# The last two attention iterations and the routing of batches 0 and 1 in another order, and GpSimd leaving its branch one step earlier

## The chip, the cores and the metric

The kernel runs on one core of a Trainium2 chip. The metric is the device time of one execution in microseconds (us). The time quoted for a kernel is the median of several executions, and one further execution is recorded by the hardware profiler; its span is the time from the first to the last instruction.

## The reference

One transformer layer over 16 batches of 256 tokens and 128 features, in float32. An attention block with a small MLP is followed by a mixture of 32 experts of which each token takes 4:

```python
h = layernorm(x) * (1 + ca) + sa
xn = rms_norm(h, ln1_w); q, k, v = xn @ Wq, xn @ Wk, xn @ Wv       # q, k normalised per head, 16 heads of 8
attn = softmax((einsum('bqhd,bkhd->bhqk', q, k) + rel_bias) * scale, causal)
y = einsum('bhqk,bkhd->bqhd', attn, v) @ Wo + h
z = relu(rms_norm(y, ln2_w) @ W1) @ W2                              # 128 -> 512 -> 128
x = x + ga * (z + y)
h = layernorm(x) * (1 + cb) + sb
scores = sigmoid(h @ gate_w.T)                                      # 32 experts
ids = top_k(scores + e_bias, 4); w = scores[ids] / sum(scores[ids])
x = x + gb * sum_k w_k * ((silu(h @ w1[e]) * (h @ w3[e])) @ w2[e])
```

## The kernel before

The program gives each of the five engines one instruction list, written by hand in program order, and the lists meet only at semaphores. An engine that waits holds up everything behind it in its own list. The order of calls in the source is the order of execution.

The work has four stages.

**Attention.** One call of `sequence(b, ...)` on each engine handles one batch of 16. The scores of a batch come as eight units (two heads each), issued by TensorE in four `pair` calls; VectorE adds the bias (`add_pair`, line 1528), ScalarE exponentiates (`exp`, line 857), and TensorE multiplies by V in four `products` calls. The context is transposed (`ctx_T`, line 1173), divided by the softmax sum on VectorE (`normalize`, lines 1553 and 1555), transposed again (`yn_T`, line 1179), multiplied by Wo (`y_out`, line 1186) and added to h (`y_rows`, line 1561). The last iterations carry work for the next stage too: with `left` = 1 (batch 14) and `left` = 0 (batch 15) they run the MLP of batches 0 and 1. `q_heads` (line 1519) spreads the queries of the next batch into the buffers that the scores read, out of the PSUM bank that `qk_T` (lines 1118 and 1122) fills and that `ctx_T` overwrites.

**MLP and routing, by turns.** For each batch: `m_transposes` (line 1194), `m_evac` on ScalarE (line 880), `hidden` (line 1200), `relu` (line 884), `mlp_out` on TensorE (line 1212) and then `mlp_out` on VectorE (lines 1583 to 1593), which ends in the layer-norm statistics. Then `normal` (line 891), `row_transposes` (line 1221), `modulated` (line 898), `scores` (line 1229), `scored` (line 906, the array `th`), `pick` on VectorE (lines 1761 to 1791, whose mask is made by line 1777), `ranks` on TensorE (line 1302, which counts how many earlier tokens went to each expert), `place` on VectorE (lines 1801 to 1807, the row numbers `posi`), and `copies` on ScalarE (lines 916 and 918). Batches 0 to 3 are handled outside the loop of turns: 0 and 1 in the last attention iterations and the stretch behind them, 2 and 3 in that stretch and the first turn. `all_turns` begins on TensorE with the `m_transposes` of batch 4.

**Scatter.** GpSimd writes each token's row four times into the experts' regions in HBM with indirect DMAs (`scatter`, line 789): 8 for each batch, 128 in all, in the order of batches. It starts a batch when `posi` and `copies` of it are there.

**Experts.** SyncE loads sorted rows (line 494) once the scatters of batches 0 to 11 have landed and the rows of padding behind each expert are written (line 1011 on ScalarE's queue holds the last eight of these, behind all of ScalarE's turns). Then 48 steps run on all engines, GpSimd scatters the results (line 809), and at the end four results for each token are gathered and summed (line 1452 and on).

Attention of GpSimd and VectorE stands in an If/Else on a flag computed from the data (`big`). The unguarded half runs here; the guarded half, which subtracts a row maximum, lies behind it in the code and is jumped over at the end. `first_stats(b)` (lines 696 to 727) is 20 small instructions of GpSimd that turn the statistics of batch 0 or 1 into the scale and shift that `normal` reads.

The experts' weights (3.1 MB) are loaded by SyncE (lines 455 and 456) into the memory of the attention bias as soon as the last `add_pair` is done.

## Time and profile before

| | us |
|---|---|
| median of 3 executions | 613.33 |
| lowest and highest of them | 606.31, 613.96 |
| the profiled execution | 605.55 |
| its span | 603.8 |

The profiled execution took 1.75 us more than its span, and lies at the lower end of the executions. In the span TensorE was busy 82%, VectorE 73%, GpSimd 65%, ScalarE 55%. Attention lasts until about 240 us, the turns until 376 us, the experts' steps until 577 us, and the sums of the end take the rest.

### The profile page before, as it was taken

The numbers are of one execution on the slowest core, as the hardware profiler recorded it, in microseconds if no ns is written. First come the engines' busy times: TensorE is split into PE (matmuls) and PEld (weight loads), VectorE is DVE, ScalarE is ACT, GpSimd is POOL, SyncE is SP. The second block draws the span as 40 slices with busy tenths as digits, with TensorE's granted clock in tenths as the row PEclk, the third lists the DMA queues.
The fourth block names the chain that finished last, engine by engine and source line by source line (L and its number), as shares of the span: only waits on it lengthen the run. The fifth ranks groups of instructions, "written<-read, shape, count | busy, mean of one in ns | idle before, by whom it ended". The sixth has DMA issues, their size and how long they took to land.

```text
span 603.8 us, 16378 instructions
## 1 busy us (share of the span) xinstructions
PE 495.3 (82%) x4570; PEld 395.8 (66%) x4571; DVE 440.8 (73%) x1484; ACT 329.7 (55%) x757; POOL 394.9 (65%) x633
## 2 busy tenths in 40 slices
PE   2479999999999988778877723489589999999876
PEld 0256666666666666667666622378588999899765
DVE  5888878887898875648899987456346666666658
ACT  1257888888788866455555523255345656444300
POOL 6477666666775452365777777777777777777730
PEclk9589999999999999998898875599779999999979
DMA  7999800000000001611111129666656545555857
GB/s 209 301 319 286 237 0 0 0 0 0 0 1 2 3 1 32 206 54 41 55 60 60 61 93 125 195 173 177 97 162 165 141 132 143 145 138 138 331 202 242
DMA packets 85298, 71.34 MB, mean 118 GB/s; under 512 B 11010, under 2 KB 78825, under 8 KB 85241
## 3 DMA queue, kind: packets, MB, share of 16 engines
q1 hardware_dynamic: 67384, 48.04, 30.3%
q0 software_dynamic: 8192, 17.84, 8.8%
q10 hardware_dynamic: 9664, 4.79, 2.7%
q8 instruction: 25, 0.41, 0.3%
q14 instruction: 33, 0.26, 0.2%
HBM read 41.12 MB, written 32.66 MB: 122 GB/s over the span
## 4 chain that ended last, share of the span: by engine, by line
PE 42%; DVE 21%; issue 14%; SPq 10%; ACT 4%; DVEq 4%; DMA 2%; POOL 1%; ACTq 0%; POOLq 0%
PE PS L1135 8%; PE PS L1157 5%; SPq L494 5%; PE PS L1200 4%; PE PS L1212 4%; SPq L463 3%; PE PS L1109 3%; DVE yidx L1931 3%; PE PS L1138 3%; PE PS L1162 2%; ACT hid L884 2%; PE PS L1186 2%; DVEq L370 2%; PE PS L1118 1%; DVE YQ L1929 1%
## 5 line engine op out<-in xcount | busy, mean ns | idle before, releaser
L809 POOL DMA_INDIRECT ys<-YQ,yidx x128 | 122.8, 959 | 40.9 <-issue 34.1
L1528 DVE TENSOR_TENSOR L<-PS,BIAS 128x768 f32<-128x768 f32 x128 | 116.3, 950 | 26.4 <-PE PS L1138 23.6
L857 ACT ACTIVATE PR<-L 128x768 f32<-128x768 f32 x128 | 105.7, 842 | 37.7 <-DVE L L1528 37.1
L1929 DVE SCALAR_TENSOR_TENSOR YQ<-PS,tag,YQ 128x128 f32 x192 | 67.3, 351 | 61.2 <-DVE yidx L1931 35.9
L789 POOL DMA_INDIRECT xs<-YQ,posi x64 | 62.4, 975 | 36.3 <-issue 28.3
L1381 PE MATMUL PS<-BIAS,V 128*128 x384 | 76.9, 345 | 4.2 <-issue 1.7
L1381 PEld LDWEIGHTS PS<-BIAS,V 128*128 128x128 f32 x384 | 63.8, 196 | 12.4 <-issue 12.4
L1135 PE MATMUL PS<-YQ 32*128 32x256 f32 x512 | 61.5, 435 | 5.6 <-DVE L L1528 4.3
L1016 ACT ACTIVATE L<-PS 128x384 f32<-128x384 f32 x48 | 23.6, 491 | 70.6 <-PE PS L1381 70.6
L789 POOL DMA_INDIRECT xs<-modb,posi x48 | 46.2, 963 | 14.6 <-issue 13.7
L1212 PE MATMUL PS<-w2s,hid 128*128 128x128 f32 x256 | 33.7, 286 | 14.3 <-ACT hid L884 14.2
L1135 PEld LDWEIGHTS PS<-YQ 32*128 32x128 f32 x512 | 29.8, 186 | 22.1 <-issue 15.3
L1212 PEld LDWEIGHTS PS<-w2s,hid 128*128 128x128 f32 x256 | 30.6, 196 | 19.0 <-ACT hid L884 19.0
L1373 PE MATMUL PS<-ident,PR 128*128 128x128 f32 x192 | 31.0, 287 | 14.6 <-DMA PR<-xs 9.7
L1157 PE MATMUL PS<-PR,V 128*32 128x256 f32 x512 | 41.3, 394 | 0.7 <-DVE YQ L1561 0.6
L1138 PEld LDWEIGHTS PS<-YQ 32*128 32x128 f32 x512 | 38.4, 190 | 2.1
L1029 ACT ACTIVATE V<-PS 128x512 f32<-128x512 f32 x48 | 28.7, 597 | 19.9 <-PE PS L1373 13.6
L1200 PE MATMUL PS<-RAW,w1s 128*128 128x256 f32 x128 | 36.7, 437 | 2.0 <-ACT RAW L880 2.0
L1138 PE MATMUL PS<-YQ 32*128 32x128 f32 x512 | 37.9, 273 | 0.0
L1373 PEld LDWEIGHTS PS<-ident,PR 128*128 128x128 f32 x192 | 24.7, 148 | 17.4 <-DMA PR<-xs 11.4
L657 POOL TENSOR_SCALAR V<-RAW,rs 128x128 f32<-128x128 f32 x32 | 24.4, 770 | 16.0 <-PE PS L1162 11.1
L884 ACT ACTIVATE hid<-PS 128x1024 f32<-128x1024 f32 x16 | 16.4, 1025 | 31.1 <-PE PS L1200 31.0
(324 smaller groups left out, 1150.3 us busy)
## 6 DMA issues: line engine op xcount, KB each, us to landing
PR<-xs SPq DMA_DIRECT2D x192, 72.0 KB
xs<-pad_row SPq DMA_DIRECT2D x1, 4608.0 KB, 25.0
xs<-pad_row SPq DMA_DIRECT2D x57, 72.0 KB, 20.2
dist_rep<-dist_row SPq DMA_DIRECT2D x4, 768.0 KB, 7.7
modb<-ys SPq DMA_DIRECT2D x6, 512.0 KB, 6.8
BIAS<-ys SPq DMA_DIRECT2D x6, 512.0 KB, 4.9
X<-in_x ACTq DMA_DIRECT2D x4, 512.0 KB, 5.8
BIAS<-dist_rep SPq DMA_DIRECT2D x4, 512.0 KB, 7.7
```

Of the source, the lines that this page charges most:

```text
L789: pool.indirect_dma_start(out=xs, out_offset=bass.IndirectOffsetOnAxis(ap=posi[j][:, t * TOPK + k:t * TOPK + k + 1], axis=0), in_=ROWS[j][ ...
L809: pool.indirect_dma_start(out=ys, out_offset=bass.IndirectOffsetOnAxis(ap=yidx[:, n:n + 1], axis=0), in_=YQ[:, n * D:(n + 1) * D], in_offs ...
L857: act.activation(PR[u % 4][:, :], L[u % 2][:, :], ACT.Exp).then_inc(s["exp_done"], 1)
L1135: pe.matmul(bank(S_A + quad, SEQ), KT[par][r, 0:P], QM[par][r, j, :], start=True, stop=True)
L1138: last = pe.matmul(bank(S_A + quad, P, SEQ), KT[par][r, P:SEQ], QM[par][r, j, P:SEQ], start=True, stop=True)
L1157: pe.matmul(o, v_flat[par][:, 0, first + 32 * j:first + 32 * j + 32], pr[:, (j % 2) * HW:(j % 2) * HW + SEQ], start=g % 2 == 0, stop=False ...
L1200: last = pe.matmul(bank(at_ + ch // 2, SEQ, (ch % 2) * SEQ), w1s[:, ch * P:(ch + 1) * P], mT[n % 2], start=True, stop=True)
L1212: last = pe.matmul(z_bank(b, n, t), hid[n % 2][:, ch, t * P:(t + 1) * P], w2s[:, ch, :], start=(ch == 0), stop=(ch == HID // P - 1))
L1373: last = pe.transpose(bank(buf % 2, P, j * P), xg[buf][:, j, 0:P], ident[:, :])
L1381: last = pe.matmul(bank(2 + 2 * par + j // 2, 2 * INNER, (j % 2) * 2 * INNER), xgT[par][:, j * P:(j + 1) * P], w13[:, bass.ds(e * (2 * INN ...
L1528: return dve.tensor_tensor(L[u % 2][:, :].rearrange("p (j w) -> p j w", j=2), PS[:, at:at + 2, 0:HW], BIAS[:, u, :].rearrange("p (j w) -> ...
L1929: dve.scalar_tensor_tensor(to, bank(6 + par, D, k * D), tag[buf][:, k, 0:1], to, ALU.mult, ALU.add)
```

## The change

The source is written in another order at the end of attention, and one call moves out of a branch; no instruction is added or removed in the path that runs, and every instruction keeps its shape. The diff (context cut):

```diff
@@ gpsimd, sequence
-                if left <= 1:
-                    first_stats(1 - left)
+                if left == 1:
+                    first_stats(0)
@@ gpsimd, behind the If/Else
             with pool.Else():
                 attention(True)
+            first_stats(1)
@@ scalar, sequence
+                if left == 0:
+                    act.wait_ge(s["qkt_done"], 2 * NB)
+                    normal(0, 0, 0)
                 exp(b, 2)
                 exp(b, 3)
                 if left >= 1:
                     qk_heads(b + 1, 1 - par)
-                else:
-                    act.wait_ge(s["qkt_done"], 2 * NB)
-                    normal(0, 0, 0)
...
                 if not first:
                     yn_T(b - 1)
+                if left == 0:
+                    act.wait_ge(s["h_kept"], NB)
+                    modulated(0, 0)
                 exp(b, 6)
...
                 else:
-                    act.wait_ge(s["h_kept"], NB)
-                    modulated(0, 0)
+                    scored(0, 0)
                 exp(b, 7)
@@ scalar, behind attention
-            scored(0, 0)
+            normal(1, 1, 1)
+            copies(0, 0)
             m_evac(2, 2)
-            copies(0, 0)
             context(NB - 1, 1)
-            normal(1, 1, 1)
+            modulated(1, 1)
             relu(2, 2)
+            scored(1, 1)
+            copies(1, 1)
+            m_evac(3, 3)
             yn_T(NB - 1)
             act.activation(LM, zero[:, :].to_broadcast([P, UW]), ACT.Copy)
-            m_evac(3, 3)
-            routed(1, 1)
             relu(3, 3)
-            copies(1, 1)
@@ tensor, sequence
                 if left <= 1:
                     mlp_out(1 - left, 1 - left)
+                    pair(b, par, 2)
                     pe.wait_ge(s["m_tev"], 2 - left)
...
-                if not first:
+                if not first and left > 1:
                     pair(b, par, 2)
...
+                if left == 0:
+                    scores(0, 0)
                 if left >= 1:
                     pair(b + 1, 1 - par, 0)
                 products(b, par, 2)
...
-                if left == 0:
-                    scores(0, 0)
@@ tensor, behind attention (the waits)
-            pe.wait_ge(s["r_th"], 1)
-            pe.wait_ge(s["h2_copies"], 1)
+            pe.wait_ge(s["r_th"], 2)
+            pe.wait_ge(s["h2_copies"], 2)
@@ vector, sequence
-                if left >= 1:
+                if left >= 2:
                     q_heads(b + 1, 1 - par)
                 if left <= 1:
                     mlp_out(1 - left, 1 - left, 1 - left)
                 if not first:
                     add_pair(b, 2, guarded)
+                if left == 1:
+                    q_heads(b + 1, 1 - par)
@@ vector, behind attention
             pick(0, 0)
             place(0, 0)
-            normalize(NB - 1)
             mlp_out(2, 2, 0)
-            y_rows(NB - 1)
             pick(1, 1)
             place(1, 1)
+            normalize(NB - 1)
+            y_rows(NB - 1)
             mlp_out(3, 3, 1)
```

In the program of after all line numbers are higher by 1 to 6.

**TensorE, iteration of batch 14 (`left` = 1).** Rows of the order, before; L1212 is the MLP of batch 0, L1157 and L1162 are `products`, L1118 and L1122 `qk_T`, L1135 and L1138 `pair`.

```order
L1212 MATMUL PS<-w2s,hid0 128x128 x8
L1157 MATMUL PS<-PR0,V0 32x256 x2
L1157 MATMUL PS<-PR1,V0 32x256 x2
L1162 MATMUL PS<-PR0,V0 32x128 x2
L1162 MATMUL PS<-PR1,V0 32x128 x2
L1118 MATMUL PS<-ident,QKN 128x128 x4
L1122 MATMUL PS<-ident,QKN 128x128 x2
L1135 MATMUL PS<-YQ 128x256 x2
L1138 MATMUL PS<-YQ 128x128 x2
L1135 MATMUL PS<-YQ 128x256 x2
L1138 MATMUL PS<-YQ 128x128 x2
```

And after:

```order
L1215 MATMUL PS<-w2s,hid0 128x128 x8
L1138 MATMUL PS<-YQ 128x256 x2
L1141 MATMUL PS<-YQ 128x128 x2
L1138 MATMUL PS<-YQ 128x256 x2
L1141 MATMUL PS<-YQ 128x128 x2
L1160 MATMUL PS<-PR0,V0 32x256 x2
L1160 MATMUL PS<-PR1,V0 32x256 x2
L1165 MATMUL PS<-PR0,V0 32x128 x2
L1165 MATMUL PS<-PR1,V0 32x128 x2
L1121 MATMUL PS<-ident,QKN 128x128 x4
L1125 MATMUL PS<-ident,QKN 128x128 x2
```

The score pair of units 4 and 5 moves from behind `qk_T` to directly behind the MLP of batch 0; the same move is made one iteration later.

**TensorE, behind attention.** Before: `ctx_T` of batch 15 (L1173), the MLP of batch 2 (L1212 with hid0), `m_transposes` of batch 3 (L1194), `yn_T` (L1179), `hidden` of batch 3 (L1200), `y_out` (L1186), routing of batch 1 (L1221, L1229, L1233), the MLP of batch 3 (L1212 with hid1), and the first of six rows of `ranks` of batch 1 (L1302).

```order
L1173 MATMUL PS<-ident,YT 128x128 x4
L1212 MATMUL PS<-w2s,hid0 128x128 x8
L1194 MATMUL PS<-ident,YQ 128x128 x2
L1179 MATMUL PS<-ident,YN 128x128 x2
L1200 MATMUL PS<-RAW1,w1s 128x256 x4
L1186 MATMUL PS<-wo,YNT 128x128 x2
L1221 MATMUL PS<-ident,QKN 128x128 x2
L1229 MATMUL PS<-gateT,hsq 128x32 x2
L1233 MATMUL PS<-ident,hsq 128x128 x2
L1212 MATMUL PS<-w2s,hid1 128x128 x8
L1302 MATMUL PS<-OH0,rest 128x32 x4
```

After (the routing of batch 1 stands ahead of these rows, beside the `hidden` of batch 2):

```order
L1176 MATMUL PS<-ident,YT 128x128 x4
L1197 MATMUL PS<-ident,YQ 128x128 x2
L1306 MATMUL PS<-OH0,rest 128x32 x4
L1306 MATMUL PS<-OH0,onesb 128x32 x4
L1306 MATMUL PS<-OH0,rest 128x32 x4
L1306 MATMUL PS<-OH1,tri 128x32 x4
L1306 MATMUL PS<-OH1,onesb 128x32 x4
L1306 MATMUL PS<-OH1,tri 128x32 x4
L1182 MATMUL PS<-ident,YN 128x128 x2
L1203 MATMUL PS<-RAW1,w1s 128x256 x4
L1189 MATMUL PS<-wo,YNT 128x128 x2
L1215 MATMUL PS<-w2s,hid1 128x128 x8
```

`ranks` of batch 1, last before, now stands ahead of `yn_T`, of `hidden` of batch 3, of `y_out` and of the MLP of batch 3, which is now last before the turns.

**VectorE, behind attention.** Before, from the end of `place` of batch 0: `normalize` of batch 15 (L1553, L1555), the MLP step of batch 2 (L1583 to L1593), `y_rows` of batch 15 (L1561), then `pick` of batch 1 (from L1761).

```order
L1807 SCALAR_TENSOR_TENSOR posi0<-nt1,rk 128x8
L1553 RECIPROCAL rden<-PS 128x32
L1555 TENSOR_TENSOR YN<-PS,rden 128x256
L1583 SCALAR_TENSOR_TENSOR XH<-PS,rstd,YQ 128x128 x2
L1587 TENSOR_TENSOR XH<-XH,modb 128x256
L1590 TENSOR_TENSOR X<-X,XH 128x256
L1593 BN_STATS stats<-X 128x6 x2
L1561 TENSOR_TENSOR YQ<-PS,YQ 128x256
L1761 TENSOR_SCALAR score<-th1 128x64
```

After:

```order
L1813 SCALAR_TENSOR_TENSOR posi0<-nt1,rk 128x8
L1587 SCALAR_TENSOR_TENSOR XH<-PS,rstd,YQ 128x128 x2
L1591 TENSOR_TENSOR XH<-XH,modb 128x256
L1594 TENSOR_TENSOR X<-X,XH 128x256
L1597 BN_STATS stats<-X 128x6 x2
L1767 TENSOR_SCALAR score<-th1 128x64
L1769 TENSOR_TENSOR sel<-score,ebias 128x64
L1772 MAX top<-sel 128x8 x2
L1776 MAX_INDEX topi<-top,sel 128x8 x2
L1780 TENSOR_SCALAR nt1<-topi 128x8
L1783 TENSOR_TENSOR OH1<-iota_v,nt1 128x256
```

`normalize` and `y_rows` of batch 15 now come behind the whole of `pick` and `place` of batch 1; `pick` of batch 1 still stands behind the MLP step of batch 2.

## Rows read from the trace of the kernel before

**Rows 1.** The chain of waits: start us, us, what, in order of time

```profile
212.95 2.05 PE PS L1212 x16
...
253.58 2.96 PE PS L1212 x16
...
257.18 0.52 PE PS L1194 x2
...
376.66 0.37 ACTq L1011
...
382.25 0.37 SPq L494
...
577.52 6.02 PE PS L1452 x16
```

**Rows 2.** TensorE in order of time: start us, us, what, [idle before <-releaser]

```profile
218.19 0.66 PE L1173 MATMUL PS<-ident,YT 128*128 128x128 f32 x4
220.33 0.70 PE L1135 MATMUL PS<-YQ 32*128 32x256 f32 x4 [1.48 <-DVE L L1528]
...
222.04 0.44 PE L1179 MATMUL PS<-ident,YN 128*128 128x128 f32 x2
...
241.29 1.99 PE L1200 MATMUL PS<-RAW,w1s 128*128 128x256 f32 x8
...
244.40 2.05 PE L1212 MATMUL PS<-w2s,hid 128*128 128x128 f32 x16
...
248.41 1.99 PE L1200 MATMUL PS<-RAW,w1s 128*128 128x256 f32 x8 [1.48 <-ACT RAW L880]
...
288.45 3.58 PE L1200 MATMUL PS<-RAW,w1s 128*128 128x256 f32 x8
```

**Rows 3.** VectorE in order of time, same columns

```profile
216.63 0.69 DVE L1519 TENSOR_TENSOR YQ<-PS,hmask 128x510 f32<-128x510 f32 x1 [2.44 <-PE PS L1122]
217.24 0.60 DVE L1583 SCALAR_TENSOR_TENSOR XH<-PS,rstd,YQ 128x128 f32<-128x128 f32 x2
...
219.32 1.82 DVE L1528 TENSOR_TENSOR L<-PS,BIAS 128x768 f32<-128x768 f32 x2
...
238.11 0.42 DVE L1561 TENSOR_TENSOR YQ<-PS,YQ 128x256 f32<-128x256 f32 x1
241.32 0.20 DVE L1761 TENSOR_SCALAR score<-th 128x64 f32<-128x64 f32 x1 [2.78 <-ACT th L906]
...
242.79 0.42 DVE L1777 TENSOR_TENSOR OH<-iota_v,nt 128x256 bf16<-128x256 f32 x1
...
245.54 0.17 DVE L1807 SCALAR_TENSOR_TENSOR posi<-nt,rk 128x8 int32<-128x8 f32 x1
...
246.49 0.61 DVE L1583 SCALAR_TENSOR_TENSOR XH<-PS,rstd,YQ 128x128 f32<-128x128 f32 x2
```

**Rows 4.** ScalarE in order of time, same columns

```profile
240.14 0.23 ACT L906 ACTIVATE th<-PS 128x64 f32<-128x64 f32 x1 [0.91 <-PE PS L1229]
```

**Rows 5.** GpSimd in order of time, same columns

```profile
219.36 0.20 POOL L696 TENSOR_TENSOR mean_g<-stats 128x2 f32<-128x2 f32 x1 [2.47 <-DVE stats L1593]
...
224.36 0.20 POOL L727 TENSOR_TENSOR nmr_g<-mean_g,rstd_g 128x2 f32<-128x2 f32 x1
...
249.55 1.21 POOL L789 DMA_INDIRECT xs<-YQ,posi  x1 [10.60 <-issue]
...
275.25 0.97 POOL L789 DMA_INDIRECT xs<-YQ,posi  x1 [5.51 <-DVE posi L1807]
...
286.81 0.96 POOL L789 DMA_INDIRECT xs<-YQ,posi  x1 [1.56 <-ACT modb L918]
```

**Rows 6.** Stretches: width, busy PE PEld DVE ACT POOL, clock, DMA share, GB/s

```profile
241.00:249.00 8.00, 6.34 (x59) 5.03 (x52) 6.61 (x26) 4.51 (x10) 0.00 (x0) 1.00 1.03 318
```

**Rows 7.** Stretches of 2 us, same columns

```profile
254.00:256.00 2.00, 2.00 (x14) 2.00 (x13) 1.79 (x7) 0.55 (x2) 1.53 (x2) 0.63 0.13 42
256.00:258.00 2.00, 1.69 (x29) 1.23 (x28) 0.80 (x3) 0.27 (x1) 1.56 (x2) 0.52 0.21 74
```

More of the change, by code:

```diff
@@ L1344, in _ @@
             pe.wait_ge(s["l_ready"], NB * UNITS + 2)
+            pe.wait_ge(s["yt_ready"], 2 * NB - 1)
+            row_transposes(1, 1, 1)
+            ranks(0, 0)
             hidden(2, 2)
-            pe.wait_ge(s["yt_ready"], 2 * NB - 1)
-            ranks(0, 0)
-            pe.wait_ge(s["r_th"], 1)
-            pe.wait_ge(s["h2_copies"], 1)
+            scores(1, 1)
+            mlp_out(2, 2)
+            pe.wait_ge(s["r_th"], 2)
+            pe.wait_ge(s["h2_copies"], 2)
             ctx_T(NB - 1)
-            mlp_out(2, 2)
             m_transposes(3, 3)
+            ranks(1, 1)
             yn_T(NB - 1)
@@ L1355, in _ @@
             y_out(NB - 1)
-            row_transposes(1, 1, 1)
-            scores(1, 1)
             mlp_out(3, 3)
-            ranks(1, 1)
             all_turns(pe, turn)
```

## The prediction

> **What bounds the kernel now.** I read the chain of waits first. Around the change it runs through TensorE with short visits to VectorE and ScalarE: the MLP of batch 3 at 253.58, and at 257.18 the first instruction of the turns [rows 1]. From there it stays among TensorE, VectorE and ScalarE until the turns end, passes to ScalarE's queue at 376.66 (rows of padding that wait behind ScalarE's turns) and at 382.25 to SyncE's first loads of sorted rows; then the experts' steps run until the sums of the end at 577.52 [rows 1]. Apart from a few us that the trace puts down to issue, nothing between 257.18 and 376.66 waits for something outside the three engines, so a shift of the first row of the turns is a shift of the end. The question is one number: when does `m_transposes` of batch 4 start, now 257.18?
>
> The second view is GpSimd's own order in time, since its scatters must also have landed before SyncE loads. It starts them at 249.55, is out of work before 275.25 (5.51 us idle, waiting for the row numbers of batch 2), and again before 286.81 (1.56 us, waiting for the copies of batch 3) [rows 5]. Behind that it is never idle again for more than the 0.3 us between two issues until the last steps. So its long queue is timed by batch 3, which the turns make, and not by batches 0 and 1. It ends batch 11 about as late as ScalarE's padding; both hang on the start of the turns, and both move with it.
>
> **GpSimd leaves the branch earlier.** Now its last instruction of `first_stats(1)` ends at 249.55 - 10.60 = 238.95. The row numbers of batch 0 are there at 245.54 + 0.17 = 245.71 [rows 3], and the first scatter starts only at 249.55 [rows 5], 3.8 us later. In between the weights of the experts fill the DMA engines (share 1.03 from 241 to 249) [rows 6]. Leaving at about 222.3 (224.36 + 0.20, less the 2.1 us of the next part), in a quiet stretch, should let the first scatter follow the row numbers at once: 4 us earlier for batch 0, and for batch 1 the same or more. Worth at the end: nothing, because batch 2 finds GpSimd idle anyway, with 5.51 us to spare [rows 5]. The cover is that idle time; it would be gone only if the turns started over 5 us earlier.
>
> What could it cost? If leaving takes the whole 10.6 us of [rows 5], it is back at 232.9, just when the statistics of batch 1 are made, and its 5.2 us of work (219.36 to 224.56) [rows 5] end at 238.1, before ScalarE wants them at about 239. So 0, and at the upper end each further us of return is a us late, since `normal(1)` now stands ahead of `copies(0)` and of the `m_evac` of batch 2 on ScalarE. I take 0: the row to which it is nearest, VectorE's own exit (2.78 us) [rows 3], is far shorter.
>
> The Trainium skill bears on this ("Runtime: NRT & Kernel Launch", section "Instruction fetch mechanics"): a taken branch whose target lies outside the blocks already held makes the engine fetch by DMA before it goes on. The trace agrees in kind, since the exit at 238.95 fell into the loaded stretch and took longest. By that rule the return is quicker than 10.6 us and the term above stays 0.
>
> **The iterations of batches 14 and 15.** Now VectorE idles 2.44 us for `qk_T` before `q_heads` at 216.63, and its MLP step starts at 217.24 although TensorE had finished at 212.95 + 2.05 = 215.0 [rows 1, 3]. With `q_heads` moved back the step starts at 215.05, 2.1 us earlier, ends at 217.1 (it takes 219.32 - 217.24 = 2.08), and the two bias adds (1.82) end at 218.95. Then `q_heads` comes (0.69), until 219.65. TensorE cannot profit in full: `ctx_T` overwrites the bank that `q_heads` reads and waits for it, so it runs from 219.7 instead of 218.19, until 220.35 (0.66). Now the fourth score pair runs from 220.33 to 222.04 in two halves, each waiting for its bias add (1.48 us idle ahead of the first) [rows 2]. After, both adds are done and the halves overlap: one half's 0.86, until 221.2. Gain: 222.04 - 221.2 = **0.85 us**. In the iteration of batch 15 TensorE's order brings nothing more that I can find, because the bias adds of unit 5 still end behind the MLP step; the 0.85 is kept. So `y_rows` of batch 14, now done at 238.11 + 0.42 = 238.53 [rows 3], is done at about 237.65.
>
> **Behind attention.** Here I follow the three lists instruction by instruction.
> - `th` of batch 0, now ready at 240.37 [rows 4], comes some 2 us earlier, but VectorE starts `pick` only 2.78 us after its last attention instruction [rows 3], and 0.95 us after `th`: what it waited for was its own exit from the branch. After: 237.65 + 2.8 = 240.4. The mask takes 242.79 + 0.42 - 241.32 = 1.9, so it stands at 242.3.
> - `ranks(0)` now stands ahead of `hidden(2)` on TensorE, and it needs that mask. With 0.3 for it (half of the 0.64 between 256.54 and 257.18 [rows 1]), `hidden(2)` starts at 242.65 instead of 241.29: **+1.35**. The MLP of batch 2 follows as now, 3.1 us later, at 245.75 instead of 244.40 [rows 2], until 247.8.
> - VectorE's step of batch 2 (2.08) runs 247.85 to 249.95. Only then comes `pick(1)`: mask at 251.85. TensorE meanwhile has done `ctx_T` (0.66) and `m_transposes(3)` (0.25) by 248.7 and stands at `ranks(1)` for **3.1 us**; it ends at 252.5.
> - VectorE ends `pick` and `place` of batch 1 at 249.95 + 4.4 = 254.35 (241.32 to 245.71 now), `normalize` takes 0.8 (245.71 to 246.49) [rows 3], and `yn_T` of TensorE, which stands ahead of `hidden(3)`, waits until 255.15: **2.6 us** idle. With its 0.4 (0.44 for the like at 222.04), `hidden(3)` runs 255.5 to 257.5 (1.99), where it now starts at 248.41 [rows 2].
> - `relu` 1.1, so the MLP of batch 3 starts at 258.6 instead of 253.58, and takes 2.05 at the full clock instead of the 2.96 of [rows 1]. It is the last before the turns and ends at 260.65.
>
> Against 257.18: **+3.5 us**. Gained beside it are the idle 1.48 us before `hidden(3)` [rows 2] and the later waits for the routing of batch 1; they are in the sum, being replaced by the two longer ones.
>
> **The clock.** Granted was 0.63 and 0.52 in the stretches from 254 to 258 [rows 7], half clock for most of them, and the MLP at 253.58 took 2.96 against 2.05 [rows 1, 2]. At the low level of 1.2 GHz a `hidden` took 3.58 instead of 1.99 [rows 2]. After, TensorE has nearly 6 us idle between 248.7 and 255.15, more than ahead of the fall now, so either `hidden(3)` or the MLP of batch 3 or both run slow: +0.9 to +2.5. I take the lower half, since a fall that comes here may be one that does not come in the turn behind. The Trainium skill ("TensorE: Matmul & The Clock Gate", part 1) has the throttled level as the default that activity releases; the trace agrees in that both falls follow idle. By that rule alone the high end, +6.0, would be the sum.
>
> **The sum.** 3.5 and some 0.5 of the clock: +4.0 us, with the ends at +2.2 (below) and +6.0. On the profiled execution 605.55 gives 609.6; on the median, 613.33 gives **617.3**. The change is 0.65%; a measurement of this kernel tells about 2% from no change, and its executions before lie 1.2% apart.
>
> **Rivals.**
> - *The tail wins instead.* Routing batch 1 early was idle time of TensorE before: 1.48 us ahead of `hidden(3)` and some 1.7 more behind it. If the mask of batch 1 were there when TensorE reaches `ranks(1)`, the turns would start at 257.18 - 0.85 - 3.1 - 0.9 (full clock) = 252.3: -4.9, or 608.4. It decides at VectorE: the mask would have to come by 248.7, and that needs `pick(1)` ahead of the MLP step of batch 2, which the order of rows denies. For it speaks only that my step times are off by 3 us in sum. Chance 0.12; faster than 2% never.
> - *VectorE's exit costs nothing.* The 2.78 us would have been the wait for `th` after all. Then `pick(0)` starts at 238.2, and TensorE is held by `copies(0)` instead until 241: +2.2, or 615.5. Chance 0.13.
> - *GpSimd returns late.* Each us beyond 12 after leaving delays `normal(1)` and all behind it on ScalarE and TensorE. A second fetch as long as the first (10.6) would give +10 more: 627. For it speaks that the scatter loop behind is another jump; against it, that this jump comes behind `first_stats(1)`. Chance 0.05.
> - *It shifts nothing.* The +4 is taken up later, where SyncE's queue and GpSimd's scatters interlock: 613.3. Against it: both start from the turns. Chance 0.1.
> - The forecast, +3.3 to +6.0: 0.6.
>
> **Range and chances.** The executions before lie between 606.31 and 613.96, and the median after may fall at either level. Low end: 606.31 with little shift, 606.5. High end: 613.96 + 6 and some, 621. Faster by over 2% would need 601.1, slower 625.6: 0.01 and 0.03, within 2% 0.96.
>
> **What the profile after would show.** First scatter near 245, right behind the row numbers of batch 0; idle before batch 2's scatter of about 15 us. TensorE waiting about 3 us for the mask of batch 1 and 2 to 3 us for `normalize` of batch 15. `hidden(3)` at 255 or later, `m_transposes(4)` near 261, the padding of ScalarE's queue near 380.5, the sums of the end near 581. Wrong I would be if the turns start before 258, or if they start at 261 and SyncE's first load is still at 382.

## The result, and the profile after

| | before | after |
|---|---|---|
| median, us (6 executions each) | 609.6 | 619.74 |
| lowest and highest | 606.31, 613.96 | 616.96, 622.99 |
| ratio of the two, with its 95% interval | | 1.0184 [1.0149, 1.0218] |
| the profiled execution | 605.55 | 619.86 |
| its span | 603.8 | 618.1 |
| mean granted clock of TensorE | 0.914 | 0.899 |

The change makes the kernel slower by 1.8%, which is 11.2 us of 609.6 (9.1 to 13.3) by the ratio; the two medians alone lie 10.1 us apart. The forecast was +4.0 us. The time lies inside the range that was given, and the direction was right; the size was not.

The two profiled executions already lie 1.7 us apart at a point that no changed instruction has reached: TensorE's MLP of batch 0 starts at 212.95 before and at 214.68 after. So I measure everything from that point. The end of the changed part is the start of the turns, `m_transposes` of batch 4.

| us after TensorE's MLP of batch 0 | before | after | difference |
|---|---|---|---|
| `hidden` of batch 1 | 12.33 | 14.67 | +2.34 |
| MLP of batch 1 | 16.60 | 18.93 | +2.33 |
| `hidden` of batch 2 | 28.34 | 33.14 | +4.80 |
| MLP of batch 2 | 31.45 | 37.87 | +6.42 |
| MLP of batch 3 | 40.63 | 52.02 | +11.39 |
| start of the turns | 44.07 | 53.91 | +9.84 |

Of the 9.84 us, 2.33 are lost by the MLP of batch 1, so in the iteration of batch 14, and 7.51 behind it. The forecast had -0.85 and +4.35 for the two.

**The iteration of batch 14.** VectorE of after in order of time: start us, us, instruction, idle before it and its releaser.

```profile
214.10 1.82 DVE L1532 TENSOR_TENSOR L<-PS,BIAS 128x768 f32<-128x768 f32 x2 [1.91 <-PE PS L1141]
218.75 0.61 DVE L1587 SCALAR_TENSOR_TENSOR XH<-PS,rstd,YQ 128x128 f32<-128x128 f32 x2 [2.83 <-POOLq L688]
...
220.83 1.82 DVE L1532 TENSOR_TENSOR L<-PS,BIAS 128x768 f32<-128x768 f32 x2
222.57 0.68 DVE L1523 TENSOR_TENSOR YQ<-PS,hmask 128x510 f32<-128x510 f32 x1
```

GpSimd of after, the last instruction ahead of that release:

```profile
218.39 0.20 POOL L685 TENSOR_TENSOR rstd<-rstd,st 128x8 f32<-128x8 f32 x1
```

TensorE of after behind it:

```profile
223.39 0.63 PE L1176 MATMUL PS<-ident,YT 128*128 128x128 f32 x4 [3.40 <-DVE YQ L1523]
...
226.65 1.11 PE L1189 MATMUL PS<-wo,YNT 128*128 128x128 f32 x4
```

Read from the top: VectorE stands for 2.83 us at its MLP step of batch 0, 2.0 of them behind the end of TensorE's MLP (214.68 + 2.05 = 216.73), and is released by a semaphore of GpSimd's sequencer. This is `yr_ready`: the step multiplies by reciprocal square roots (`rstd`) which GpSimd makes in 14 small instructions (`y_roots`, L674 to L685) in this iteration, and the first such step waits for them. They end at 218.59. Behind the step stand the bias adds and now `q_heads` too, which ends at 223.25; `ctx_T` overwrites the bank that `q_heads` reads, and TensorE stands there for 3.40 us. Before, it ran at 218.19 without a wait [rows 2]. After the stand, `y_out` took 1.11 us (before 0.71).

The trace of before holds the explanation, in a stretch of GpSimd that I did not look at ahead of the prediction:

```profile
216.69 0.20 POOL L685 TENSOR_TENSOR rstd<-rstd,st 128x8 f32<-128x8 f32 x1
```

The roots ended at 216.89, the MLP step started at 217.24 [rows 3]. `q_heads` in front of the step covered this wait completely. The step never could have started at 215.05.

**Behind attention.** VectorE of after:

```profile
245.54 0.20 DVE L1767 TENSOR_SCALAR score<-th 128x64 f32<-128x64 f32 x1 [2.94 <-issue]
...
249.77 0.17 DVE L1813 SCALAR_TENSOR_TENSOR posi<-nt,rk 128x8 int32<-128x8 f32 x1
254.64 0.61 DVE L1587 SCALAR_TENSOR_TENSOR XH<-PS,rstd,YQ 128x128 f32<-128x128 f32 x2 [4.70 <-PE PS L1215]
...
258.19 0.42 DVE L1783 TENSOR_TENSOR OH<-iota_v,nt 128x256 bf16<-128x256 f32 x1
```

TensorE of after:

```profile
247.50 0.27 PE L1306 MATMUL PS<-OH,tri 128*128 128x32 bf16 x4 [1.66 <-DVE OH L1783]
...
247.82 3.62 PE L1203 MATMUL PS<-RAW,w1s 128*128 128x256 f32 x8
...
252.55 2.05 PE L1215 MATMUL PS<-w2s,hid 128*128 128x128 f32 x16 [0.46 <-ACT hid L885]
...
258.67 0.29 PE L1306 MATMUL PS<-OH,rest 128*128 128x32 bf16 x4 [3.42 <-DVE OH L1783]
...
261.89 0.69 PE L1182 MATMUL PS<-ident,YN 128*128 128x128 f32 x2 [2.39 <-DVE YN L1559]
262.37 3.22 PE L1203 MATMUL PS<-RAW,w1s 128*128 128x256 f32 x8
...
266.70 2.05 PE L1215 MATMUL PS<-w2s,hid 128*128 128x128 f32 x16 [0.67 <-ACT hid L885]
268.59 0.38 PE L1197 MATMUL PS<-ident,YQ 128*128 128x128 f32 x2
```

The two waits that were forecast are there: 3.42 us for the mask of batch 1 and 2.39 us for `normalize` of batch 15. Beside them, `hidden` of batch 2 takes 3.62 us and that of batch 3 takes 3.22, where both took 1.99 before [rows 2]. The stretches of after show why: width, busy time of PE, PEld, DVE, ACT and POOL, granted clock, DMA share, GB/s.

```profile
246.00:248.00 2.00, 0.50 (x13) 0.50 (x14) 1.79 (x10) 0.44 (x1) 0.00 (x0) 1.00 1.09 347
248.00:250.00 2.00, 2.00 (x6) 1.56 (x6) 1.77 (x7) 0.00 (x0) 0.00 (x0) 0.50 1.09 324
...
256.00:258.00 2.00, 0.00 (x0) 0.00 (x0) 1.79 (x12) 0.00 (x0) 1.43 (x2) 1.00 0.21 74
...
260.00:262.00 2.00, 0.11 (x1) 0.12 (x2) 1.73 (x6) 0.00 (x0) 1.01 (x2) 0.50 0.22 74
262.00:264.00 2.00, 2.00 (x6) 1.72 (x7) 0.00 (x0) 1.11 (x2) 1.69 (x2) 0.50 0.12 39
```

TensorE was busy 0.50 us of the 2 us from 246, and from 248 the grant is 0.50, which is the 1.2 GHz level; it was busy for nothing of the 2 us from 256 and 0.11 of those from 260, and the second `hidden` runs at 0.50 too. In return the MLP of batch 3 runs at the full clock, 2.05 us against 2.96 [rows 1].

**GpSimd** of after, the first scatters of batches 0, 1, 2 and 3:

```profile
250.96 1.21 POOL L790 DMA_INDIRECT xs<-YQ,posi  x1 [7.98 <-issue]
...
261.95 0.95 POOL L790 DMA_INDIRECT xs<-YQ,posi  x1 [0.79 <-DVE posi L1813]
...
286.53 0.97 POOL L790 DMA_INDIRECT xs<-YQ,posi  x1 [14.57 <-DVE posi L1813]
...
297.76 0.95 POOL L790 DMA_INDIRECT xs<-YQ,posi  x1 [1.24 <-ACT modb L919]
```

The first scatter follows the row numbers (249.94) by 1.0 us instead of 3.8, and then GpSimd idles 14.57 us ahead of batch 2.

**Carried to the end.** Chain of waits of after:

```profile
388.65 0.37 ACTq L1014
...
393.71 0.37 SPq L494
...
592.17 1.19 PE PS L1456 x2
```

Against [rows 1] these are +12.0, +11.5 and +14.65 us; less the 1.7 us of the two executions, the first two are 10.3 and 9.7, about the 9.8 of the changed part. The last 3 us are added in the experts' steps, and are taken up below.

### The profile page after: what moved, and what is told of

Read it like the earlier page. It is cut to its first block, busy times and chain, and to the rows that moved or that the text cites. A ratio compares the mean times of both kernels' runs of the same rounds, so it can differ in the third digit from the quotient of the medians.

```text
span 618.1 us, 16380 instructions
## 1 busy us (share of the span) xinstructions
PE 498.6 (81%) x4570; PEld 399.1 (65%) x4571; DVE 439.9 (71%) x1484; ACT 329.2 (53%) x757; POOL 395.2 (64%) x633
## 4 chain that ended last, share of the span: by engine, by line
PE 41%; DVE 24%; issue 15%; SPq 6%; DVEq 5%; ACT 4%; DMA 3%; another core or an unknown queue 1%; POOL 1%; ACTq 0%; POOLq 0%
PE PS L1138 8%; PE PS L1160 5%; PE PS L1203 5%; PE PS L1215 4%; DVE yidx L1937 3%; PE PS L1112 3%; PE PS L1141 3%; SPq L494 3%; PE PS L1165 2%; SPq L463 2%; DVEq L370 2%; ACT hid L885 2%; DVE YQ L1935 2%; PE PS L1189 2%; PE PS L1121 2%
## 5 line engine op out<-in xcount | busy, mean ns | idle before, releaser
L1935 DVE SCALAR_TENSOR_TENSOR YQ<-PS,tag,YQ 128x128 f32 x192 | 67.3, 350 | 63.2 <-DVE yidx L1937 35.8
L1385 PE MATMUL PS<-BIAS,V 128*128 x384 | 78.2, 349 | 10.3 <-issue 8.3
L1138 PE MATMUL PS<-YQ 32*128 32x256 f32 x512 | 61.1, 438 | 4.3 <-DVE L L1532 3.5
L790 POOL DMA_INDIRECT xs<-modb,posi x48 | 46.3, 964 | 14.6 <-issue 13.7
L1138 PEld LDWEIGHTS PS<-YQ 32*128 32x128 f32 x512 | 29.6, 187 | 20.5 <-issue 15.7
L1203 PE MATMUL PS<-RAW,w1s 128*128 128x256 f32 x128 | 38.3, 453 | 0.5 <-ACT RAW L881 0.5
L1141 PE MATMUL PS<-YQ 32*128 32x128 f32 x512 | 37.6, 274 | 0.0
L657 POOL TENSOR_SCALAR V<-RAW,rs 128x128 f32<-128x128 f32 x32 | 24.8, 781 | 16.1 <-PE PS L1165 11.2
```

The costliest lines, as they stand in the source:

```text
L790: pool.indirect_dma_start(out=xs, out_offset=bass.IndirectOffsetOnAxis(ap=posi[j][:, t * TOPK + k:t * TOPK + k + 1], axis=0), in_=ROWS[j][ ...
L1138: pe.matmul(bank(S_A + quad, SEQ), KT[par][r, 0:P], QM[par][r, j, :], start=True, stop=True)
L1141: last = pe.matmul(bank(S_A + quad, P, SEQ), KT[par][r, P:SEQ], QM[par][r, j, P:SEQ], start=True, stop=True)
L1203: last = pe.matmul(bank(at_ + ch // 2, SEQ, (ch % 2) * SEQ), w1s[:, ch * P:(ch + 1) * P], mT[n % 2], start=True, stop=True)
L1385: last = pe.matmul(bank(2 + 2 * par + j // 2, 2 * INNER, (j % 2) * 2 * INNER), xgT[par][:, j * P:(j + 1) * P], w13[:, bass.ds(e * (2 * INN ...
L1935: dve.scalar_tensor_tensor(to, bank(6 + par, D, k * D), tag[buf][:, k, 0:1], to, ALU.mult, ALU.add)
```

## The experiments

Each kernel was run beside the kernel before on its own chip, and the ratios are to that. On the chips of the eight runs marked * everything, the kernel before too, took some 780 us instead of 610. Once GpSimd's scatters run there, ScalarE and VectorE wait for something that the trace names only as `remote`, another core or an unknown queue. The first such wait of the eight traces is at 258.4 us, so of these runs I use the trace ahead of it, the tails with care, and the time as a ratio to before. "To MLP 1" is from TensorE's MLP of batch 0 to that of batch 1; "tail" is from there to the start of the turns.

| kernel | to MLP 1 | tail | both | ratio of times [95%] |
|---|---|---|---|---|
| before | 16.60 | 27.47 | 44.07 | 1 |
| after | 18.93 | 34.98 | 53.91 | 1.0184 [1.0149, 1.0218] |
| e1, e8 * GpSimd's part alone | 16.58, 16.59 | 27.44, 27.39 | 44.02, 43.98 | 0.9941 [0.9876, 1.0005], 0.9948 [0.9904, 0.9992] |
| e2, e9 * all but GpSimd's part | 19.23, 20.47 | 40.8, 37.2 | 60.1, 57.7 | 1.0208 [1.013, 1.0285], 1.0122 [1.0065, 1.0178] |
| e3 * iteration 14 undone | 17.86 | 35.8 | 53.64 | 1.0062 [1.0, 1.0124] |
| e7 * MLP step of batch 0 last | 15.86 | 37.5 | 53.38 | 0.9986 [0.9935, 1.0036] |
| e4 routing of batch 1 first | 21.61 | 30.63 | 52.24 | 1.0102 [1.007, 1.0133] |
| e5, e10 * tail undone | 18.94, 20.52 | 27.3, 27.8 | 46.3, 48.3 | 0.9989 [0.994, 1.0038], 0.9925 [0.9883, 0.9968] |
| e12 tail undone | 19.12 | 27.92 | 47.04 | 1.0053 [1.0019, 1.0088] |
| e6 before, ScalarE's tail reordered | 16.59 | 24.65 | 41.24 | 0.9991 [0.9957, 1.0024] |
| e11 both repaired | 15.86 | 24.23 | 40.09 | 0.9954 [0.9919, 0.9988] |

The kernel of after itself was not run on a chip of the marked kind.

### GpSimd's part alone (e1, e8)

The kernel before, with this alone:

```diff
-                if left <= 1:
-                    first_stats(1 - left)
+                if left == 1:
+                    first_stats(0)
...
+            first_stats(1)
```

> The kernel before, with only the move of first_stats(1) on GpSimd out of the branch. My theory (GpSimd's exit has cover on both sides): time as before, within 2 us; the first scatter follows the row numbers of batch 0 within 1.5 us instead of 3.8 us, the idle time before batch 2's scatter grows from 5.5 to 7 or 8 us, and the turns start 44.2 us after the MLP of batch 0, as before. Rival (the move itself makes the kernel slower, through a late normal(1) or a second fetch): some of the 10 us of the whole change appear here, and ScalarE waits for first_stats(1).

> The same kernel as e1_pool_alone (the kernel before with only GpSimd's move), since the chip of the first call ran every kernel, the one before too, at some 780 us. My theory: as before within 2 us; turns start 44.1 us after the MLP of batch 0; GpSimd idle about 8 us before batch 2's scatter. Rival (an earlier first scatter is worth something at the end): 2 to 4 us faster.

The changed stretch stays where it was (44.02 and 43.98 against 44.07). GpSimd of e1:

```profile
247.50 1.21 POOL L790 DMA_INDIRECT xs<-YQ,posi  x1 [7.81 <-issue]
...
279.76 0.97 POOL L790 DMA_INDIRECT xs<-YQ,posi  x1 [8.93 <-DVE posi L1808]
```

The idle time ahead of batch 2 is 8.93 us instead of 5.51 [rows 5]: what the early exit gains is given back there. The times are 0.6% and 0.5% below before, of which only the second interval leaves out 1, barely, on chips where the scatters meet waits that the normal ones don't have. The exit is worth nothing in the stretch, and about half a per cent in time, if anything, on such a chip.

### Everything but GpSimd's part (e2, e9)

The change, with `first_stats(1)` back in the branch.

> The changed kernel with only first_stats(1) put back into the branch. My theory: still 9 to 11 us slower than before, as the whole change; the first scatter comes later but finds the turns late anyway. Rival (the exit is what costs): most of the 10 us goes away.

> The same kernel as e2_pool_back (the changed kernel with first_stats(1) back in the branch). On the slow chip it was the slowest of four and its turns started at 60.1 us after the MLP of batch 0 against 53.9 in the changed kernel, but waits of unknown origin disturbed that stretch. My theory: as the changed kernel, +9 to +11 us, turns at 53.9. Rival (in the new order normal(1) or the scatters depend on GpSimd's early exit): turns at 56 or later, +13 or more.

The first scatter is late again. GpSimd of e2:

```profile
252.97 1.21 POOL L789 DMA_INDIRECT xs<-YQ,posi  x1 [10.62 <-ACT YQ L918]
```

So the idle time over the exit is 10.6 us as in the kernel before, and it ends 3.9 us behind the row numbers (249.02) instead of 1.0. The tails of 40.8 and 37.2 us hold waits of VectorE for `remote` (2.46 us ahead of `place` of batch 1, 6.68 ahead of `y_rows` in e2), so their size says nothing about the normal chip. In time the two are 16 us (10 to 22) and 9.6 us (5 to 14) above before, where 9 to 11 was expected. What stands is that the order of the other engines loses its time without GpSimd's part as well.

### The iteration of batch 14 (e3, e7)

e3 puts TensorE's score pair and VectorE's `q_heads` of batch 14 back where they were. e7 keeps TensorE's new order and puts VectorE's MLP step last:

```diff
-                if left <= 1:
+                if left == 0:
                     mlp_out(1 - left, 1 - left, 1 - left)
                 if not first:
                     add_pair(b, 2, guarded)
                 if left == 1:
                     q_heads(b + 1, 1 - par)
+                    mlp_out(0, 0, 0)
```

> The changed kernel with the iteration of batch 14 back in its old order (score pair of units 4 and 5 behind qk_T, q_heads ahead of VectorE's MLP step). Theory 1 (in that iteration VectorE's MLP step of batch 0 cannot start earlier, because it waits for GpSimd's roots of the second norm, and q_heads, now queued behind it, holds back ctx_T): 2.3 us from that iteration come back and the dip of the clock there goes; total 2 to 4 us faster than the changed kernel, hidden of batch 1 starts 12.4 us after the MLP of batch 0 instead of 14.7. Rival (as predicted, that iteration gains 0.85 us by the new order, and all is lost in the tail): the time gets worse by 0.9 us or stays.

> The changed kernel with one step moved on VectorE in the iteration of batch 14: bias adds of units 4 and 5, then q_heads, then the MLP step of batch 0 (changed: MLP step first, which waits 2.8 us for GpSimd's roots with the other two queued behind it). Theory (that wait, not the order on TensorE, is what costs in this iteration): ctx_T's wait of 3.4 us falls to about 0.5 us, hidden of batch 1 starts 12.3 to 13.3 us after the MLP of batch 0 instead of 14.7, total 1 to 2.5 us faster than the changed kernel. Rival (the early score pair on TensorE delays qk_T and is the cost): hidden of batch 1 stays at 14 us or later.

In e3 every wait up to 222.5 is that of before again: TensorE reaches `ctx_T` without one.

```profile
218.67 0.66 PE L1176 MATMUL PS<-ident,YT 128*128 128x128 f32 x4
220.80 0.70 PE L1138 MATMUL PS<-YQ 32*128 32x256 f32 x4 [1.48 <-DVE L L1533]
```

`hidden` of batch 1 starts 13.60 us after the MLP of batch 0, where 12.4 was expected, and the MLP of batch 1 comes 1.26 us later than before (17.86), because here the clock fell right behind (`yn_T` 0.61 us instead of 0.44), with the same instructions and the same waits in front of it as before. So in this one profile about half of the 2.33 us is restored by the order, and the rest is a fall of the clock that this order can also have. The other profiles with the order of before show no such fall: before, e1, e6 and e8 have 16.58 to 16.60 us to MLP 1. All seven with the changed order of VectorE (after, e2, e4, e5, e9, e10, e12) have 18.93 to 21.61.

In e7 the MLP step starts behind `q_heads` without a wait, and `ctx_T` waits 0.24 us instead of 3.40. VectorE of e7:

```profile
220.52 0.68 DVE L1523 TENSOR_TENSOR YQ<-PS,hmask 128x510 f32<-128x510 f32 x1
221.12 0.60 DVE L1587 SCALAR_TENSOR_TENSOR XH<-PS,rstd,YQ 128x128 f32<-128x128 f32 x2
```

TensorE of e7:

```profile
221.38 0.63 PE L1176 MATMUL PS<-ident,YT 128*128 128x128 f32 x4 [0.24 <-ACT YQ L850]
```

`hidden` of batch 1 starts 11.60 us after the MLP of batch 0, against 12.33 before and 14.67 after. This is the test of the cause: with the same TensorE order, moving the one step that waits for the roots behind the two that others wait for turns a loss of 2.33 us into a gain of 0.74. It is not free: `normalize` now stands behind the MLP step, and TensorE waits 1.26 us for it at `yn_T`. e11 has the same order and the same 15.86 us to MLP 1. The tails of e3 and e7, 35.8 and 37.5 us, hold 2.5 us each of a wait for `remote` ahead of `place` of batch 1, so they are near the 35.0 of after or below it; the times (1.0062 and 0.9986, on different chips) do not tell a us.

### Routing of batch 1 ahead of the MLP step of batch 2 (e4)

The change, with VectorE's tail in this order:

```diff
-            mlp_out(2, 2, 0)
             pick(1, 1)
             place(1, 1)
             normalize(NB - 1)
+            mlp_out(2, 2, 0)
```

> The changed kernel with VectorE's order behind attention altered again: pick and place of batch 1 and normalize of batch 15 ahead of the MLP step of batch 2 (TensorE and ScalarE stay as changed). Theory: TensorE's wait for the mask of batch 1 (3.4 us) falls to 1 us or less, since th of batch 1 is there 2.2 us before the MLP step of batch 2 starts, and its wait for normalize of batch 15 (2.4 us) falls to about 1 us: the turns start 50 us after the MLP of batch 0 instead of 53.9, total 3 to 5 us faster than the changed kernel and still 4 to 7 slower than before. Rival (the waits only move elsewhere, onto z_done for the MLP of batch 3 or onto the late start of hidden of batch 2): the turns start at 53 us or later, no gain.

TensorE of e4:

```profile
256.73 0.25 PE L1306 MATMUL PS<-OH,rest 128*128 128x32 bf16 x4
...
259.54 0.69 PE L1182 MATMUL PS<-ident,YN 128*128 128x128 f32 x2 [2.06 <-DVE YN L1559]
260.02 3.27 PE L1203 MATMUL PS<-RAW,w1s 128*128 128x256 f32 x8
```

The wait of 3.42 us at `ranks` of batch 1 is gone and the tail is 4.35 us shorter (30.63 against 34.98); the turns start at 52.24, between the 50 expected and the 53 of the rival. The second wait stays: `normalize` comes behind `place` of batch 1, which needs these `ranks`, so TensorE stands 2.06 us at `yn_T`, and `hidden` runs at the low clock (3.27). In this run the iteration of batch 14 cost more (21.61 to MLP 1), since behind the 3.40 us stand at `ctx_T` the low clock lasted until `hidden` of batch 1 (2.63 us instead of 1.99). The time is 6.2 us above before (4.3 to 8.1), where after was 11.2.

### The tail undone (e5, e10, e12)

The changed iterations and GpSimd's exit, with the orders of before on TensorE, ScalarE and VectorE behind attention. It was run three times, since the first two runs fell on the chips of 780 us.

> The changed kernel with the stretch behind attention back in the order of before, on TensorE, ScalarE and VectorE; the two attention iterations and GpSimd stay as changed. Theory: only the loss of the iteration of batch 14 is left, 2 to 3 us slower than before; the 7 us of the stretch behind attention come back. Rival (the iterations are harmless, the tail alone counts): as before, 0 us. Rival 2 (the iterations make it all, by pushing the exits of VectorE and GpSimd into the load of the experts' weights): 8 to 10 us slower than before.

> The same kernel as e5_tail_before (iterations and GpSimd as changed, the stretch behind attention as before). In the profile on the slow chip the MLP of batch 1 came 18.9 us after that of batch 0 (16.6 before, 18.9 changed) and the turns at 46.3 (44.1 before, 53.9 changed). Theory: +2 us over before in time, so that the stretch behind attention is worth 8 of the 10 us. Rival (time lost in the iterations is taken up, or the slow clock there comes and goes): 0.

> The changed iterations of batches 14 and 15 and GpSimd's early exit, with the tail in the order of before: the same kernel as the tail put back twice already, whose times came from chips on which every kernel ran long. Theory (of the 10 us lost, about 2 come from the iteration of batch 14 and 7 to 8 from the tail): the MLP of batch 1 18.9 us after that of batch 0 (before 16.6), turns' start 46.3 after it (before 44.1), the time 2 us above that of before. Rival, the earlier scatters take up the iteration's loss: the same stretches, the time within 1 us of before or below it. Rival, the tail is not the cause: 8 to 10 us above before.

e12 ran on a normal chip: 611.93 us beside 609.8, ratio 1.0053, which is +3.2 us (1.2 to 5.4) by the ratio and 2.1 by the medians. Its stretch is 2.97 us longer than that of before: 2.52 up to MLP 1 and 0.45 in the tail. TensorE of e12:

```profile
223.00 1.00 PE L1175 MATMUL PS<-ident,YT 128*128 128x128 f32 x4 [3.40 <-DVE YQ L1522]
...
257.22 3.67 PE L1214 MATMUL PS<-w2s,hid 128*128 128x128 f32 x16 [0.98 <-ACT hid L885]
```

The stand at `ctx_T` is that of after, 3.40 us. The 0.45 of the tail is the sum of a loss and a gain. The MLP of batch 3 took 3.67 us where it took 2.96 before, and some 0.4 us more were lost ahead of it. Against that, `hidden` of batch 2 starts 11.08 us after the MLP of batch 1 instead of 11.74. The same 11.07 or 11.08 stand in e5, e10 and e11, and 11.74 in before, e1, e6 and e8, so the changed iteration of batch 15 gains 0.66 us. TensorE there has `scores` of batch 0 to do where it stood 0.61 us for `y_rows`:

```profile
238.68 0.64 PE L1157 MATMUL PS<-PR,V 128*32 128x256 f32 x8 [0.61 <-DVE YQ L1561]
```

This row is of the kernel before; e12 has no wait at its like. The loss of the iteration of batch 14 thus reaches the end, and the earlier scatters do not take it up. The rest of the change's 11.2 us, 8.0 (some 3 us either way, from the two intervals), belongs to the new order of the tail (6.9 in the stretches: 53.91 against 47.04).

On the chips of 780 us this kernel came out level with before (0.9989) and 0.75% below it (0.9925), although its stretch was 2.2 and 4.3 us longer. That does not fit with e12, and I have no account of it beyond GpSimd's part being slightly favourable there.

### ScalarE's order (e6), and both repairs together (e11)

e6 is the kernel before with two moves in ScalarE's tail, which had made TensorE wait 1.48 us ahead of `hidden` of batch 3 [rows 2]:

```diff
+            m_evac(3, 3)
             yn_T(NB - 1)
             act.activation(LM, zero[:, :].to_broadcast([P, UW]), ACT.Copy)
-            m_evac(3, 3)
-            routed(1, 1)
             relu(3, 3)
+            routed(1, 1)
             copies(1, 1)
```

e11 is e12 with e7's order of VectorE and e6's order of ScalarE.

> The kernel before with one thing altered on ScalarE behind attention: m_evac of batch 3 ahead of yn_T of batch 15 and of the fill of the maximum buffer, and relu of batch 3 ahead of the routing of batch 1. Theory: TensorE's 1.48 us ahead of hidden of batch 3 go, but relu(3) ahead of modulated(1) delays the scores of batch 1 by about 1 us, which TensorE has ahead of the MLP of batch 3; in sum the turns start 43 us after the MLP of batch 0 instead of 44.2, total 1 to 2 us faster than before. Rival (the start of the turns does not set the end): unchanged within 0.5 us.

> Changed iterations of batches 14 and 15, but with VectorE's MLP step of batch 0 behind its pair sum and its query heads, GpSimd early; the tail in the order of before, with ScalarE evacuating batch 3's mean ahead of its yn_T and LM fill, and relu(3) ahead of routed(1). Theory (the changed order's loss in the iteration is VectorE's MLP step waiting for GpSimd's y_roots; the tail is limited by VectorE and ScalarE's order): hidden(1) 11.6 us and the MLP of batch 1 15.9 us after TensorE's MLP of batch 0 (before 12.3 and 16.6), turns' start 40.5 us after it (before 44.1), the time 2 to 4 us below that of before. Rival, the tail of before has slack further on that takes up such gains (the ScalarE order alone took 2.8 us from this stretch and the median stood still): turns' start as early, the time within 1 us of before. Second rival, the clock falls where TensorE is fed later: hidden(2) or hidden(3) at 3.2 to 3.6 us instead of 2.0, turns' start at 43 to 44, no gain.

TensorE of e6, `hidden` and MLP of batch 3:

```profile
248.81 1.99 PE L1200 MATMUL PS<-RAW,w1s 128*128 128x256 f32 x8 [0.25 <-ACT RAW L880]
...
253.09 1.95 PE L1212 MATMUL PS<-w2s,hid 128*128 128x128 f32 x16
```

The wait falls from 1.48 to 0.25 us and, with less idle time ahead of it, the MLP of batch 3 runs at full clock (1.95 against 2.96). The turns start 2.83 us earlier, yet the medians are 608.97 and 609.08. The interval is -2.6 to +1.5 us: it holds no gain at all, and the whole 2.83 lies just outside it. In the profiled execution, the fastest of the twelve, 2.6 of the 2.8 us are still there at the sums of the end (361.95 us after the MLP of batch 0 against 364.57). How much of the gain the usual execution keeps stays open.

e11 has the shortest stretch of all, 40.09 us, 4.0 below before. TensorE of e11:

```profile
246.74 1.99 PE L1202 MATMUL PS<-RAW,w1s 128*128 128x256 f32 x8
...
251.02 1.95 PE L1214 MATMUL PS<-w2s,hid 128*128 128x128 f32 x16
```

Its median is 606.25 us beside 609.8, ratio 0.9954 [0.9919, 0.9988]: 2.8 us faster than before (0.7 to 4.9) by the ratio, 3.6 by the medians, and some 2.3% faster than after, each taken against before on its own chip. It holds GpSimd's exit and the new TensorE order of batches 14 and 15, so these do no harm in themselves; what made the change slower is where VectorE's MLP step of batch 0 stands, and the tail.

### What stays open in the experts' steps

From SyncE's first load to the sums of the end the profiles have 195.3 us (before), 195.1 (e6), 195.1 (e11), but 198.5 (after), 198.5 (e4) and 197.9 (e12). In this stage GpSimd's scatters of results run back to back, 1.26 us each, and all six profiles keep that pace until the last sixteen. What is longer behind that are waits of GpSimd for row numbers of VectorE. Before:

```profile
577.55 0.96 POOL L809 DMA_INDIRECT ys<-YQ,yidx  x1 [2.14 <-DVE yidx L1931]
```

After, there are two:

```profile
578.74 0.96 POOL L810 DMA_INDIRECT ys<-YQ,yidx  x1 [2.07 <-DVE yidx L1937]
...
592.21 0.95 POOL L810 DMA_INDIRECT ys<-YQ,yidx  x1 [3.68 <-DVE yidx L1937]
```

So some of VectorE's row numbers come late in after. Above the pace these waits come to 1.8 us before, 5.6 after and 3.9 in e12. They are not the whole of the difference, for e11 has one as well and its stage is no longer than that of before:

```profile
575.20 0.96 POOL L810 DMA_INDIRECT ys<-YQ,yidx  x1 [3.30 <-DVE yidx L1937]
```

In e11 the scatters begin 35.4 us behind SyncE's first load, before 36.7 and in e12 37.6. No experiment addressed why. e12, whose stretch moved by 3 us only, has the longer stage too, so it does not go with the size of the shift.

## Why the prediction was right in direction and short in size

- **What bounds the end.** Right. The first row of the turns moved by 11.6 us (257.02 to 268.59 in TensorE's own rows), the padding of ScalarE's queue by 12.0 and SyncE's first load by 11.5. The rival "it shifts nothing" fell: e12's 3.0 us of stretch came out as 3.2 by the ratio.
- **GpSimd leaves earlier: 0.** Right, by its own steps: the first scatter 1.0 us behind the row numbers, 14.57 us idle ahead of batch 2 where about 15 was given, and a stretch that did not move in e1 and e8. GpSimd was back from the early exit in time: its `first_stats(1)` started at 237.83, right behind VectorE's statistics, and ended 0.4 us ahead of `normal` of batch 1. The profile also counts the packets of a DMA queue of the kind `instruction` (q14). Between GpSimd's two `first_stats` it has two of them after and in e1, e8 and e11, at 227 and 229 us in after, and none before, in e2 and in e9. With the late exit the last ones come at 245 and 247 us before and at 248 and 250 in e2, the very last about 2 us ahead of the first scatter. The rival "GpSimd returns late" fell with this. The Trainium skill ("Runtime: NRT & Kernel Launch", "Instruction fetch mechanics") states that a taken branch whose target is not in the blocks already held must wait for a DMA fetch of it. These packets agree with that, and so does the idle time over the late exit, 10.6 us before and 10.62 in e2; how long one fetch takes no run shows.
- **The iterations of batches 14 and 15: a gain of 0.85 us.** Wrong, and the step that failed is the first one: "With `q_heads` moved back the step starts at 215.05". It took the end of TensorE's MLP (215.0) for the only thing that the step waits for. The code has two waits there, and `yr_ready` of GpSimd comes at 216.89 in that trace. After, the step started 2.83 us later than VectorE was free, `q_heads` ended at 223.25 instead of the 219.65 of the prediction, and the iteration lost 2.33 us: the term is off by 3.2 us and has the wrong sign. e7 shows the cause. The 0.85 us itself was there to be had: e7 and e11 gain 0.74. That the order brings nothing more in the iteration of batch 15 was wrong too, to the good: it gains 0.66 us in e5, e10, e11 and e12, which in after the wait for the mask of batch 0 covers.
- **Behind attention: +4.35 before the clock.** Right in mechanism and in size. From the MLP of batch 1 to `hidden` of batch 2 the steps gave +2.2 (1.35 and the 0.85), measured +2.47; VectorE's exit 2.8, measured 2.94; from the MLP of batch 2 to the mask of batch 1 6.1, measured 6.12; from there to `yn_T` 3.3, measured 3.22. The rival "VectorE's exit costs nothing" fell with the 2.94. e12 against after puts the tail at 8.0 us of the median, and e4 shows that each of the two waits has the cause named.
- **The clock: +0.5, ends 0.9 and 2.5.** Right in mechanism, under-sized. `hidden` of batch 2 took 1.63 us more and that of batch 3 1.23 more: 2.9 us, above even the high end. I had looked at the wait ahead of `hidden` of batch 3 only, and not at the 1.66 us stand at `ranks` of batch 0, of the prediction's own making, behind which the first fall came. The argument for the lower half ("a fall that comes here may be one that does not come in the turn behind") got no support: the fall ahead of the turns was indeed gone (MLP of batch 3 at 2.05), but that 0.9 was already in the sum, and from the start of the turns to SyncE's first load it is 125.1 us after as it was 125.2 before. The high end, +2.5, was nearer. The prediction's sentence on the Trainium skill ("TensorE: Matmul & The Clock Gate", part 1), that the throttled level is the default and activity releases it, pointed there; the trace agrees in that both `hidden` at the low clock follow idle time of TensorE.
- **The sum.** 3.5 forecast without the clock, 3.2 for the iteration, 2.9 for the clock and 0.2 for the small steps make 9.8, which is the stretch. The time went up by 11.2 (9.1 to 13.3) by the ratio and 10.1 by the medians, of which the experts' steps, a term that the sum did not have, hold 3.2 in the two profiles.
- **The range.** That it held was luck in part. It was built on 613.33, the median of three executions; six give 609.6. The highest shift forecast, +6.0, would make 615.6 of that, less than any of the six executions after (616.96 and up).

## What to carry to other kernels

When a step is moved to an earlier place, the wait that ends last before the move is not the one that will end last after it: list every semaphore that the step waits for in the code, and read from the trace when each of them was signalled, even where the trace shows no idle time for it. Here the step with two producers belonged behind the step that another engine waits for (e7: 0.24 us instead of 3.40 at `ctx_T` for the same move, though 1.26 at `yn_T` behind it). And where a reordering adds stands of TensorE, price the matmuls behind each of them at the low clock too: here 2.9 us on top of 5.8 us of waits. It is a price that can come or not, since a `hidden` behind 1.48 us of idle time ran at the full clock before [rows 2].

## What was not expected of the hardware

- The same kernel took some 610 us on some chips and some 787 on others (787.07 and 787.54 for before), with waits of up to 15.28 us for something that the trace cannot name, only once GpSimd's scatters run. ScalarE of e3:

```profile
325.07 1.02 ACT L885 ACTIVATE hid<-PS 128x1024 f32<-128x1024 f32 x1 [15.28 <-remote]
```

- Behind the same stand of 3.40 us at `ctx_T` the low clock lasted for different times in different runs: until `y_out` or so in after (18.93 us to MLP 1), into `hidden` of batch 1 in e4 (21.61), e9 (20.47) and e10 (20.52). One order of instructions thus has a loss of 2.3 to 5 us here, and e3, with the order of before, fell where before did not.
